# First attention layer of a gated two-layer block: each head's scores as its own 64-row product, without zero blocks in the keys

## The reference, cut to what matters

```python
HEADS, DIM_HEAD = 16, 64                     # x: (2, 1024, 256), context: (2, 154, 192)
q = (x @ Wq).reshape(B, Nq, h, dh)
k = (context @ Wk).reshape(B, Nk, h, dh)
v = (context @ Wv).reshape(B, Nk, h, dh)
scores = jnp.einsum('bqhd,bkhd->bhqk', q, k) * scale
attn = jax.nn.softmax(scores, axis=-1)
out = jnp.einsum('bhqk,bkhd->bqhd', attn, v).reshape(B, Nq, h * dh)
return out @ Wo + bo
...
x = x + jnp.tanh(g_xattn[0]) * _L0_xattn_ref(_layernorm(x, axis=-1), ctx_768, ...)
```

## Time and profile before

| | |
|---|---|
| runs | 968.0, 969.36, 969.6 us |
| profiled execution | 964.45 us, of which its span is 962.7 us (1.75 us lie around it) |
| mean granted TensorE clock | 0.967 |
| PE busy | 890.0 us, 92% of the span |
| VectorE / ScalarE / GpSimd busy | 560.2 / 521.9 / 351.5 us |
| steps of the first attention | from about 48 to 314 us of the span |

### The profile page before, as it was taken

How to read it: one execution, slowest core, us unless ns; L and a number is a source line. 1 busy time by engine, 2 the same in 40 slices (tenths; PEclk the granted TensorE clock), 3 DMA queues, 4 the chain that set the end, 5 groups by cost and what they waited for, 6 DMA issues and landing times.

```text
span 962.7 us, 19673 instructions
## 1 busy us (share of the span) xinstructions
PE 890.0 (92%) x6485; PEld 804.8 (84%) x6486; DVE 560.2 (58%) x1328; ACT 521.9 (54%) x1473; POOL 351.5 (37%) x494
## 2 busy tenths in 40 slices
PE   5789999999998888999999991799999999999996
PEld 3469999999997766999999991799999999987653
DVE  3475555556656673434434345777777777656456
ACT  7376766667766323443443453565556555652555
POOL 2263444444444113212222135655556544453000
PEclk9899999999999878999999995999999999999998
DMA  8000000060000346676777741200000000000002
GB/s 257 1 1 1 2 1 1 14 195 2 0 1 1 106 145 250 230 267 240 254 258 236 263 127 55 48 22 13 24 11 22 11 13 1 2 1 1 1 1 88
DMA packets 37570, 76.17 MB, mean 79 GB/s; under 512 B 5166, under 2 KB 23842, under 8 KB 37378
## 3 DMA queue, kind: packets, MB, share of 16 engines
q1 hardware_dynamic: 34097, 66.03, 20.7%
q0 software_dynamic: 3408, 9.31, 3.0%
HBM read 66.02 MB, written 9.31 MB: 78 GB/s over the span
## 4 chain that ended last, share of the span: by engine, by line
PE 82%; DVE 7%; POOL 4%; DMA 3%; ACT 2%; issue 2%; DVEq 0%; SPq 0%; POOLq 0%
PE banks L524 15%; PE banks L526 14%; PE banks L525 14%; PE banks L1444 14%; PE banks L559 7%; PE banks L550 6%; PE banks L414 3%; PE banks L1709 2%; PE banks L1714 1%; PE banks L1720 1%; PE banks L1702 1%; POOL W L1120 1%; DMA region_b<-in_L_xattn_Wk 1%; PE banks L531 1%; PE banks L1434 1%
## 5 line engine op out<-in xcount | busy, mean ns | idle before, releaser
L1022 ACT ACTIVATE region_a<-banks,negmax 128x154 f32<-128x154 f32 (+1 forms) x384 | 161.8, 436 | 30.5 <-DVE negmax L834 29.6
L1444 PE MATMUL banks<-region_b,region_a 128*128 128x128 f32 x1248 | 147.5, 277 | 1.2 <-ACT region_b L1479 1.2
L1444 PEld LDWEIGHTS banks<-region_b,region_a 128*128 128x128 f32 x1248 | 144.4, 194 | 1.6 <-issue 0.9
L1145 POOL TENSOR_TENSOR region_a<-region_a,recip 128x512 f32<-128x512 f32 x64 | 66.7, 1042 | 163.5 <-PE banks L559 102.0
L834 DVE TENSOR_REDUCE negmax<-banks 128x4 f32<-128x616 f32 (+1 forms) x128 | 100.6, 786 | 39.0 <-PE banks L550 25.6
L1186 POOL TENSOR_TENSOR region_a<-region_a,recip 128x640 f32<-128x640 f32 x64 | 80.3, 1255 | 103.9 <-DVE recip L838 103.7
L1534 DVE SCALAR_TENSOR_TENSOR region_b<-banks,region_a,region_b 128x128 f32<-128x128 f32 x156 | 44.0, 345 | 109.0 <-PE banks L1444 95.9
L559 PE MATMUL banks<-ident,region_a 128*128 128x128 f32 x640 | 91.2, 273 | 7.4 <-POOL region_a L1147 3.7
L559 PEld LDWEIGHTS banks<-ident,region_a 128*128 128x128 f32 x640 | 76.3, 141 | 20.4 <-POOL region_a L1147 6.1
L524 PE MATMUL banks<-xT_high,Wq_high 128*128 128x256 f32 x256 | 79.9, 312 | 9.0 <-POOL Wq_low L1167 5.0
L1004 ACT CAST pT_high<-banks 128x640 fp32r<-128x640 f32 x64 | 44.4, 694 | 66.2 <-PE banks L559 66.2
(11 more groups left out here) (275 smaller groups left out, 2491.9 us busy)
## 6 DMA issues: line engine op xcount, KB each, us to landing
region_a<-in_L_ffn_W SPq DMA_DIRECT2D x39, 1024.0 KB, 5.0
y_slots<-region_b SPq DMA_DIRECT2D x39, 128.0 KB, 4.1
W<-in_L_ffn_W SPq DMA_DIRECT2D x1, 4096.0 KB, 14.8
xn_rows<-region_b SPq DMA_DIRECT2D x1, 2048.0 KB, 8.6
out<-x SPq DMA_DIRECT2D x8, 256.0 KB, 2.2
x<-in_x SPq DMA_DIRECT2D x1, 1536.0 KB, 12.4
region_b<-in_L_xattn_Wq SPq DMA_DIRECT2D x1, 1024.0 KB, 11.6
region_b<-in_L_xattn_Wo SPq DMA_DIRECT2D x1, 1024.0 KB, 14.2
```

Source lines behind the costliest of these rows:

```text
L1022: e = act.activation(into, source, ACT.Exp, bias=negmax[:, n % 2, u:u + 1], accum_out=sums[:, n % 2, u:u + 1])
L1145: pool.tensor_tensor(normed[:, 0:512].rearrange("p (j n) -> p j n", j=4), pr[:, :, 0:P], rc.broadcast_to([P, 4, P]), ALU.mult)
L1444: mm = pe.matmul(banks[:, 2 * r + part, m * P:(m + 1) * P], W1[r][:, k, cols], xgT[:, r, k, :], start=(k == 0), stop=(k == DK - 1))
```

## The change

`K0` keeps its shape, but both heads' keys now go to columns 0 to 153, each in its own 64 rows, and nothing is zeroed. Each product of 128 rows by 308 columns becomes two, one per head, of 64 rows by 154 columns. Head `i` of both chunks of a step writes bank `i` of the step's two, chunk `u` at columns 154u. The reduction and the exponentials read the same numbers from their new places. `k_zero` is gone.

```diff
         def head_keys(c, i):
-            return K0[64 * i:64 * i + 64, :, c, i * NKEY:(i + 1) * NKEY]
+            return K0[64 * i:64 * i + 64, :, c, 0:NKEY]
...
                 if L is L0:
-                    mm = pe.matmul(o, q0[:, c, rows], K0[:, b, c, :], start=True, stop=True)
+                    for i in range(2):
+                        half = slice(64 * i, 64 * i + 64)
+                        mm = pe.matmul(scores[:, n % 2, i, u * NKEY:(u + 1) * NKEY], q0[half, c, rows], K0[half, b, c, 0:NKEY],
+                                       start=True, stop=True)
...
-                    into, source = into.rearrange("p (u i) -> p u i", u=2), source.rearrange("p u (i n) -> p u i n", i=2)
+                    into, source = into.rearrange("p (u i) -> p i u", u=2), source.rearrange("p i (u n) -> p i u n", u=2)
...
-                dve.wait_ge(sem("k_zero"), 1)
                 dve_kv(dve, L, "k")
...
-                        source = scores[:, n % 2, u // 2, u % 2 * NKEY:(u % 2 + 1) * NKEY]
+                        source = scores[:, n % 2, u % 2, u // 2 * NKEY:(u // 2 + 1) * NKEY]
...
-                act.copy(K0.rearrange("p b c n -> p (b c n)"), zero.broadcast_to([P, 2 * NC * KEYS])).then_inc(sem("k_zero"), 1)
                 for high, low in V0:
...
-                act.wait_ge(sem("k_zero"), 1)
                 act_kv(act, L, "k")
```

## The result

The changed kernel took 958.04 us (median of four runs, 957.37 to 960.29), the one before 969.45: a ratio of 0.9888, 95% interval 0.9869 to 0.9906. That is 11 us faster, where no change beyond 0.6 us was forecast. Both are true, and why they differ is told with the clock.

The account below looks back on a forecast made before the run. TensorE was taken to bound the first attention. Per block 0.28 + 0.53 + 0.365 = 1.17 us against 1.16, times 58 steps, gave +0.6 us: 969.36 + 0.6, about 970 us, range 958 to 993.

Parts of the forecast that it names:

- What bounds the kernel: First attention: TensorE is busy nearly throughout, so its change per 4.09 us step reaches the end one for one, 58 steps.
- The start: Kernel start: dropping ScalarE's 4.30 us zeroing of the keys gains nothing; it becomes a longer wait for TensorE's first keys.
- the sum for a block: Score block, last values part to first transpose: 1.17 us with full overlap against 1.16 now, +0.01 per block.
- The middle term: Eight score matmuls within a block: row halves overlap as the order allows, four pitches of 0.13, 0.53 us with issue.
- The last term: Out of a score block to the first transpose: 0.13 us of streaming plus a 0.235 us switch, 0.365 us.
- The first term: Into a score block from the values: 0.107 us of streaming plus a 0.17 us switch to 64 rows, 0.28 us.
- Loads one after the other: Score block: streams overlap but eight weight loads pass singly at 0.112 us each; 16 us slower, 985 us; chance 27%.
- No overlap: Score block: the two row halves never run at the same time; 23 us slower, 993 us; chance 13%.
- Faster with the drains gone: Score block edges: smaller drains than in the coupling network; without drains -22 us, 947; half gone, 958; chance 15%.
- The chances: Whole kernel's outcome: faster 29%, same 16%, slower 55%.
- rivals 2 and 3: Score block: weight loads one after the other (27%, 16 us slower, 985), and no overlap at all (13%, 23 us, 993).
- That TensorE's clock falls isn't either: First attention: a falling TensorE clock was dismissed as a rival, since drains leave only a fraction of a microsecond idle.

Follow-up runs that it names:

- the changed kernel once more: The changed kernel rerun with no edit, beside the follow-up experiments and the kernel before: 961.63 us against 964.96, ratio 0.9942.
- heads-apart run: Changed kernel with its score products reordered, head 0 of both chunks, then head 1 of both: 960.93 us, ratio 0.9937 to the kernel before.
- columns-split kernel: Kernel before with each score product cut into two of 128 rows by 154 columns, zero blocks still multiplied: 968.4 us, ratio 1.0022.
- run with four switches: Changed kernel with chunk 0's score products ahead of the transposes and chunk 1's behind, in steps 1 to 6 of each pair: 974.74 us, ratio 1.0082.

## Why the prediction was wrong, by its own steps

**What bounds the kernel** held. TensorE's time in the step went into the end: 0.166 us less per step times the 58 steps that were priced in full is 9.6 us, and by clock the changed kernel is 9.3 us faster.

**The start** held: zeroing put back changes nothing. In the first trace the keys' product did start 0.77 us earlier than before (10.02 against 10.79 us), but it was released by the landing of the weights, and that moves from run to run: it started at 10.63 in the changed kernel once more, and at 10.59 with the zeroing put back. ScalarE's first copy of the keys starts at 13.06 us in the changed kernel once more, after a wait of 4.74 us, as the prediction named it (13.3, near 5).

**The step that failed is the sum for a block**, "overlap in full: 0.28 + 0.53 + 0.365 = 1.17 us". The mechanism was the forecast's: halves overlap, and two drains take back a part, 0.34 us of the 0.51 that the overlap saves in a block. Two of its three terms were too large. The table counts from stream to stream, where a stream is the time in which the columns pass:

| term | predicted us | measured us |
|---|---|---|
| last part of the values to the first score stream | 0.28 | 0.31 |
| first score stream to the last | 0.53 | 0.39 |
| last score stream to the first transpose's | 0.365 | 0.28 |
| sum, against 1.16 before | 1.17 | 0.98 |

By the plain starts of the records, which the prediction named as signs, the three are 0.21 (0.26 to 0.28 was named), 0.50 (0.53) and 0.22 (0.3 or more). The middle one looks as forecast and isn't. A matmul record that follows a switch starts with its load, before it streams: the second couple starts 0.235 us after the first and not 0.131, so the first streams 0.104 us after its start at 128.62, that is 0.31 after 128.41. From there it is three pitches of 0.131 to the last. The same holds for the first transpose, whose follower comes after 0.164 instead of 0.109: 129.34 - 129.12 + 0.055 = 0.28.

**The middle term** counted four pitches, because it let only a head's second matmul run beside the next head's first. The heads-apart run shows that the order within a block doesn't bind: all matmuls of one half pair with those of the other, so eight take four slots, three pitches from first to last. Their streams take 0.52 us instead of 1.04, half and not the 0.68 of the prediction's estimate for two halves.

**The last term** took 0.235 us from line 1720 and put the streaming of 0.13 us in front of it. But line 1720's matmuls are bound by their loads. The single records of the trace of before show it: the last of the eight starts at 916.718, its load at 916.690, and a load of 64 rows takes 0.104 us before the first column, as above. So it streams at 916.79, about 0.08 us after its record's start, and the drain was counted from a start that lay that far ahead of the stream. Read rightly, gives 0.235 - 0.08 = 0.155 behind the stream, and 0.13 + 0.155 = 0.285, which is what was measured.

**The first term** came near by luck: two errors in it cancel. It gave 0.05 us to the stream of a transpose, 128 columns, where the prediction's own rate of 0.13 us for 154 makes it 0.11, the whole pitch of 0.109. That counted 0.055 us too much as drain. And it put 0.02 us for the load that delays the first stream, which takes 0.104. The middle and the last term are 0.22 us too large together, the first 0.03 too small: 0.19 us per block, the size of the gain.

**Rivals.** Loads one after the other (27%) is refuted: two loads of different halves start 7 ns apart. No overlap (13%) is refuted, and priced: 952.3 by clock, 19 us slower than before, where 23 were given. Faster with the drains gone (15%) is refuted as a mechanism, although its side won: 48 more blocks cost 16.5 us. That its "half the drains gone would give 958" meets the measured 958.04 is luck: of the 0.40 us that the forecast gave the two switches of a block beyond the pitches of before (0.28 - 0.12 and 0.365 - 0.13) 0.34 were measured. The Trainium skill's rule that a change of tiling mode drains the engine (TensorEngine Tiling (Array Packing), "Key Properties") agrees with the traces: about 0.10 us (an estimate from the starts and the streams' lengths) lie between the end of the last stream and the next load, on either side of a block and, read in the same way, of line 1702 as well.

**The chances** put 55% on slower. The weight of rivals 2 and 3 came from no row that shows two halves at once, since the trace had none. The reason given for the overlap, that each head has a bank of its own, was not tested: no run here has both halves in one bank.

**What wasn't foreseen** is the clock. "That TensorE's clock falls isn't either" (a rival) was said of the middle of the stage, where it holds (1.00 in every stretch). At the ends of the stage the changed kernel met the lower level more often: 0.961 against 0.965 in mean, which took back some 4 of 9 us in the second set (an estimate: 0.004 of 962 us). Where TensorE was kept busy there, the mean clock rose again. Why a kernel with a shorter step meets the lower level more often than the one before, whose trace has the same waits of up to 1.5 us at the end of the stage, stays open: where in a run the stretches fall is seen in profiled runs alone, and there is one of the kernel before, without the stretch at the end, and there are two of the changed one, one with and one without it (the columns-split kernel, with the step of before, has 3.4 us there). The first comparison, 0.9888, had all four runs of before at 968.0 us or more, near its slower group, and the changed kernel's at 0.962 to 0.966; the second had it the other way, seven of nine runs of the changed kernel at 0.962 or below.

## What to carry to other kernels

Heads of 64 dimensions in both row halves of TensorE, each with a bank of its own (whether that matters wasn't tested), stream at the same time, in both orders tried within a block; zero blocks to fill the rows waste half of it. Each block of them costs about 0.34 us for switching in and out, so gather them: a block of four products of 154 columns gains 0.17 us (0.51 of overlap less 0.34), one of eight gains, by the same sum, twice that and another 0.34, if it brings no new waits, and one of two loses, as the run with four switches shows. When a drain or a pitch is taken from another place of the trace, find out first whether the records there start with the stream or with the load.

## What the runs showed of the hardware that was not expected

- Matmuls of two row halves pair up, 6 to 7 ns apart when the products change halves after every product, and still 13 to 14 ns apart when four matmuls and four loads of one half stand ahead of those of the other.
- Two float32 weight loads of 64 rows run at once (starts 6 to 7 ns apart), while those of line 1720, one product after the other, go at 0.11 us each.
- A switch between 128 and 64 rows and back costs a block 0.34 us (16.5 us for 48 of them).
- One kernel's runs on one chip differ by 5 us, 0.6%, along with the mean granted clock (0.962 or 0.968), and needless work of 2 to 3 us by clock did not lengthen the median (959.66 against 961.63 us, in two sets whose medians of before differ by 0.6).
